# The last six expert tiles in half-tiles of tokens, with the next stage's norm and queries among them, in a four-stage transformer kernel

## The chip, the cores and the metric

One core of a Trainium2 chip runs the whole kernel in one launch. TensorE multiplies matrices into PSUM, VectorE, ScalarE and GpSimd work on tiles in SBUF, and SyncE (SP) issues most of the DMA copies. Waits between them are semaphores written out by hand. The metric is device time in microseconds, lower is better.

## The reference

Two layers, each an attention and a mixture of experts, on x of 4 batches x 256 tokens x 256 channels (1,024 tokens), all in float32:

```python
x = x + L0_xattn(layernorm(x), ctx, mask)    # dense attention on 1,601 context rows per batch
x = x + L0_ffn(layernorm(x), ...)            # 16 experts of width 176, 6 per token, plus a shared one of 352
x = x + L1_xattn(layernorm(x), ctx, mask)    # 16 heads of 16: q = Wq x + bq; softmax(clip(q k / 4)) v; Wo, norm
x = x + L1_ffn(layernorm(x), ...)            # 16 experts of width 128, 2 per token, plus a shared one
```

The change lies in the second line and its passage to the third. In L0_ffn every expert is computed for every token and scaled by that token's weight, which is zero where the expert was not chosen:

```python
for e in range(E):
    g = hs @ gate_proj[e].T; u = hs @ up_proj[e].T
    inter = silu(g) * u
    out = out + comb[:, e:e + 1] * (inter @ down_proj[e].T)
```

## The kernel before

**Precision.** A float32 product is made of three matmuls of split operands: high x high, high x low, low x high (mm3). Every operand exists as a rounded high part and the remainder. ScalarE usually writes the high part and VectorE subtracts for the low one.

**The feed-forward stage (ffn).** Its weights are 25 tiles of 128 hidden units: 3 of the shared expert (sh) and 22 of the experts (ex, NEX0). A tile holds gate, up and down weights, 768 columns. SP loads it into one of two slots of w_raw, and split on VectorE makes w_hi and w_lo of it, also in two slots: a copy, then a subtraction, then w_rdy counts one up. The 1,024 tokens are taken in two halves of 512. Half a tile is one chunk, numbered ct, 50 in all. For a chunk TensorE runs gate (6 matmuls of 512 columns) into bank 4 and up (6 more) into bank 5, and then down of the chunk before it (12 matmuls of 256 columns) into banks 0 to 3, where the whole stage's output is accumulated: banks 0 and 1 for the first half of the tokens, 2 and 3 for the second. Both halves of a tile come one after the other, so the banks of both are complete only at the last chunk. ScalarE takes silu of gate and later writes hh, the high part. VectorE multiplies silu by up (L1872), multiplies by the token's weight comb_b (L1876), subtracts for the low part hl (L1878), and in the first half of each tile then splits the next tile (L1796, L1798). comb_b has two slots; SP broadcasts a tile's weights into one (L426) as soon as the products of the tile two earlier are made. The expert tiles run in hardware loops of two tiles. Beside it SP fills x_slots in DRAM from blank with 20 copies of 1 MB (L416), one in each tile.

**The passage.** tiles_add adds a pair of output banks' halves to resid, then come statistics, the root (ScalarE's Sqrt and a reciprocal), tile_norm, transposes on TensorE (pair_T), and the split into xTh and xTl. This is done for the first two batches' tokens pair by pair. The first queries, of batch 0 and the first four heads, are made by first_queries with weights repeated three times over (wgh, wgl, made in attention_weights_lo), so that ScalarE and VectorE write them in place into qst. qst holds for every head high, high and low part and a row of ones on 49 partitions. All other queries are made for 512 tokens at a time (queries), written to qh and ql, and restacked into qst by DMA copies of 16 partitions that SP issues (restack, L536: 4 for each of three parts of a group of four heads), group by group, while the attention already runs. The second half's norm and queries run between the attention's units (early). SP issues the copies of keys (keys, kst), seven for a group of four heads, and of values (vsl) after the expert loop.

**The attention.** 208 units of 128 context rows for four heads: qk (L999), an exponential on ScalarE (L1483), a clip on VectorE (L2009), pv (L1041). The qk of the first unit waits for the keys and for the first queries.

Of the kernel before, what the change touches and what calls it, by code (L numbers as in the profile page):

```python
# [15 lines left out]
F32 = mybir.dt.float32  # L16
# [29 lines left out]
WC = 3 * D  # L46
EPS = 1e-5
# [32 lines left out]
def build(nc, a, out, stop="D"):  # L80
# [9 lines left out]
    with ExitStack() as ctx:  # L90
# [47 lines left out]
        with ExitStack() as s:  # L138
            Bt = lambda name, shape, dt=F32: sbuf(s, name, shape, dt)
            w_raw = Bt("w_raw", [P, 2, WC])  # L140
# [3 lines left out]
            w_hi = Bt("w_hi", [P, 2, WC], F32R)  # L144
            w_lo = Bt("w_lo", [P, 2, WC], F32R)
            silu = Bt("silu", [P, 2, 512])
            h32 = Bt("h32", [P, 2, 512])
            hh, hl = Bt("hh", [P, 2, 512], F32R), Bt("hl", [P, 2, 512], F32R)
            logit = Bt("logit", [E, NT * P])
            comb = Bt("comb", [E, NT * P])  # L150
            comb_b = Bt("comb_b", [P, 2, NT * P])
            g_s = Bt("g_s", [P, NT, E])
            g_c = Bt("g_c", [P, NT, E])
            g_pair = Bt("g_pair", [P, NT * 4, 6])
            g_gs = Bt("g_gs", [P, NT * 4])
            g_gr = Bt("g_gr", [P, NT * 4])
            g_beats = Bt("g_beats", [P, NT, E * (E + 1)])
            g_beats4 = Bt("g_beats4", [P, NT, 4 * 5])
            bar_w = Bt("bar_w", [P, MP], I32)
            bar_i, bar_f = bar_w[0:NB, :], bar_w[0:NB, :].bitcast(F32)  # L160
            Bt("gap3b", [P, 2032 - MP])
# [4 lines left out]
            blank = Bt("blank", [P, CAP // P, XW])  # L166

        with ExitStack() as s:
            C = lambda name, shape, dt=F32: sbuf(s, name, shape, dt)
            qst = C("qst", [P, NB, NH // 2, SEQ], F32R)  # L170
            p32 = C("p32", [P, PBUF, 1024])
            qh, ql = C("qh", [P, KT, NT * P], F32R), C("ql", [P, KT, NT * P], F32R)
            oS = C("oS", [P, SEQ])
            cx = C("cx", [P, NT, D])
            s4 = C("s4", [P, 2, HG])
            r4 = C("r4", [P, 2, HG])
            wq_raw = C("wq_raw", [P, KT, D])
            wo_raw = C("wo_raw", [P, KT, D])
            wqh, wql = C("wqh", [P, KT, D], F32R), C("wql", [P, KT, D], F32R)
            wgh, wgl = C("wgh", [P, KT, 2 * P], F32R), C("wgl", [P, KT, 2 * P], F32R)  # L180
            bq = C("bq", [P, KT])
            bq0 = C("bq0", [P, 2])
# [6 lines left out]
        with ExitStack() as s:  # L189
            Dt = lambda name, shape, dt=F32: sbuf(s, name, shape, dt)  # L190
            with ExitStack() as sw:
                yg = sbuf(sw, "yg", [P, NT, 2, D])
# [3 lines left out]
            Dt("gap5", [P, 5376])  # L196
# [32 lines left out]
            nv, na = Dt("nv", [P, 2]), Dt("na", [P, 2])  # L229
# [134 lines left out]
        def inverse_root(e, b, call):  # L364

            s = slice(2 * b, 2 * b + 2)
# [9 lines left out]
            link(e.tensor_scalar(nv[:], mv[:, s, 1], EPS, None, ALU.add))  # L376
            link(e.tensor_scalar(yi, nv[:].bitcast(I32), -0.5, 1597463007.0, ALU.mult, ALU.add))
            for k in range(3):
                link(e.tensor_tensor(na[:], nv[:], y, ALU.mult))
                link(e.tensor_tensor(na[:], na[:], y, ALU.mult))  # L380
                link(e.tensor_scalar(na[:], na[:], -0.5, 1.5, ALU.mult, ALU.add))
                if k < 2:
                    link(e.tensor_tensor(y, na[:], y, ALU.mult))
            e.tensor_tensor(rstd[:, s], na[:], y, ALU.mult).then_inc(rs_rdy, 1)

        @block.sync
        def _(sp):
# [16 lines left out]
            def load_rest(f):  # L404
                for k in range(2, f["sh"] + 1):
                    tile(f, 0, k)
                for r in range(f["ex"]):
                    if r + 1 < f["ex"]:
                        tile(f, 0, f["sh"] + r + 1)
# [9 lines left out]
                    e = f["e0"] + 2 * r  # L419
                    if e >= 4:  # L420
                        sp.wait_ge(mul2_rdy, e - 2)
                    edge = -(-r * P // f["width"]) * f["width"] - r * P
# [89 lines left out]
            if stop == "B":  # L512
                return store(sp)
# [45 lines left out]
            for job in range(KSL, NJ):  # L559
# [7 lines left out]
                if job == 2 * KSL:  # L567
                    ones_rows(2 * per, NB * per, q_in[NG])
# [1839 lines left out]
```

## Time and profile before

| | us |
|---|---|
| median of three runs | 740.78 |
| lowest, highest | 739.04, 744.77 |
| the profiled execution's own time | 739.67 |
| its span from first to last instruction | 737.8 |
| TensorE busy in the span | 683.4 (93%) |
| VectorE busy | 533.0 (72%) |
| ScalarE busy | 380.3 (52%) |
| GpSimd busy | 173.3 (23%) |

A busy time is the time in which an engine works on an instruction, waits left out. Matmuls are pipelined, so one that lasts 0.40 us is followed by the next after 0.23 us. The first stage takes up to about 185 us, the feed-forward from there to about 405, the attention from 414 to 632, the last stage the rest. The time of the execution is longer than the span by what lies before the first and behind the last instruction, 1.9 us.

### The profile page before, as it was taken

The numbers are of one execution on the slowest core, as the hardware profiler recorded it, in microseconds if no ns is written. First come the engines' busy times: TensorE is split into PE (matmuls) and PEld (weight loads), VectorE is DVE, ScalarE is ACT, GpSimd is POOL, SyncE is SP. The second block draws the span as 40 slices with busy tenths as digits, with TensorE's granted clock in tenths as the row PEclk, the third lists the DMA queues.
The fourth block names the chain that finished last, engine by engine and source line by source line (L and its number), as shares of the span: only waits on it lengthen the run. The fifth ranks groups of instructions, "written<-read, shape, count | busy, mean of one in ns | idle before, by whom it ended". The sixth has DMA issues, their size and how long they took to land.

```text
span 737.8 us, 14927 instructions
## 1 busy us (share of the span) xinstructions
PE 683.4 (93%) x5499; PEld 532.1 (72%) x5499; DVE 533.0 (72%) x1176; ACT 380.3 (52%) x566; POOL 173.3 (23%) x220
## 2 busy tenths in 40 slices
PE   4899999997999999999999799999999999989990
PEld 3899999996778888888887555454454554677870
DVE  5785767677566666666666788789789888775555
ACT  3634344431423223232233699999889999434550
POOL 4562727220010000000000050004204505343561
PEclk9999999999999999999999899999999999799996
DMA  7567475714437677776769859977979640654535
GB/s 253 183 208 263 155 268 170 270 68 149 149 117 261 215 225 254 244 240 215 219 217 212 126 79 173 181 149 107 213 125 195 112 69 2 214 215 135 167 125 192
DMA packets 55274, 131.55 MB, mean 178 GB/s; under 512 B 10006, under 2 KB 36102, under 8 KB 51630
## 3 DMA queue, kind: packets, MB, share of 16 engines
q1 hardware_dynamic: 51950, 123.32, 61.7%
q0 software_dynamic: 2256, 6.18, 2.4%
q10 hardware_dynamic: 1008, 1.25, 0.5%
q8 instruction: 38, 0.62, 0.4%
q14 instruction: 22, 0.18, 0.1%
HBM read 79.09 MB, written 48.82 MB: 173 GB/s over the span
## 4 chain that ended last, share of the span: by engine, by line
PE 74%; DVE 10%; POOL 5%; ACT 5%; DMA 3%; issue 3%; SPq 0%; ACTq 0%; DVEq 0%; POOLq 0%
PE ps L692 16%; PE ps L693 15%; PE ps L694 15%; PE ps L1041 10%; PE ps L999 7%; PE ps L1229 3%; ACT p L1483 2%; DVE p L2009 2%; PE ps L1245 2%; PE ps L1063 1%; PE ps L778 1%; DMA prob<-in_ctxT 1%; PE ps L1213 1%; POOL nv L376 1%; DMA comb_b<-comb_rows 1%
## 5 line engine op out<-in xcount | busy, mean ns | idle before, releaser
L1483 ACT ACTIVATE p<-ps 128x1024 f32<-128x1024 f32 (+1 forms) x208 | 193.4, 1052 | 9.8 <-PE ps L999 9.4
L2009 DVE TENSOR_SCALAR p<-p 128x1024 f32<-128x1024 f32 (+1 forms) x208 | 138.6, 686 | 18.5 <-ACT p L1483 17.6
L1041 PE MATMUL ps<-p,vsl 128*17 128x256 f32 (+1 forms) x1664 | 116.1, 383 | 6.6 <-DVE p L2009 5.3
L1389 ACT ACTIVATE hh<-h 128x512 fp32r<-128x512 f32 x50 | 31.6, 632 | 132.9 <-DVE h L1876 115.9
L999 PEld LDWEIGHTS ps<-qst,kst 49*128 49x128 f32 (+1 forms) x832 | 57.0, 182 | 48.3 <-issue 26.1
L376 POOL TENSOR_SCALAR nv<-mv 128x2 f32<-128x2 f32 x8 | 8.9, 1116 | 351.5 <-DVE mv L1939 210.5
L999 PE MATMUL ps<-qst,kst 49*128 49x256 f32 (+1 forms) x832 | 81.6, 311 | 1.3 <-DVE qst L1952 0.9
L692 PE MATMUL ps<-xTh,w_hi 128*128 128x512 f32 x200 | 79.9, 399 | 1.5 <-DVE h L1872 0.8
L693 PE MATMUL ps<-xTl,w_hi 128*128 128x512 f32 x200 | 79.0, 395 | 0.0
L694 PE MATMUL ps<-xTh,w_lo 128*128 128x512 f32 x200 | 78.9, 395 | 0.0
L1041 PEld LDWEIGHTS ps<-p,vsl 128*17 128x17 f32 (+1 forms) x1664 | 35.4, 96 | 47.0 <-DVE p L2009 12.6
L1878 DVE TENSOR_TENSOR hl<-h,hh 128x512 fp32r<-128x512 f32 x50 | 34.6, 692 | 36.6 <-ACT hh L1389 36.6
L692 PE MATMUL ps<-w_hi,hh 128*128 128x256 f32 x200 | 56.8, 284 | 1.8 <-DVE hl L1878 1.5
L1872 DVE TENSOR_TENSOR h<-silu,ps 128x512 f32<-128x512 f32 x50 | 34.4, 688 | 31.9 <-PE ps L694 20.8
L693 PE MATMUL ps<-w_lo,hh 128*128 128x256 f32 x200 | 56.3, 281 | 0.0
L694 PE MATMUL ps<-w_hi,hl 128*128 128x256 f32 x200 | 56.2, 281 | 0.0
L692 PEld LDWEIGHTS ps<-xTh,w_hi 128*128 128x128 f32 x200 | 37.7, 189 | 9.4 <-DVE h L1872 1.7
L694 PEld LDWEIGHTS ps<-xTh,w_lo 128*128 128x128 f32 x200 | 37.6, 188 | 8.9
L693 PEld LDWEIGHTS ps<-xTl,w_hi 128*128 128x128 f32 x200 | 37.7, 189 | 6.6
L692 PEld LDWEIGHTS ps<-w_hi,hh 128*128 128x128 f32 x200 | 37.7, 188 | 5.8 <-DVE hl L1878 3.8
L1342 ACT ACTIVATE prob<-sS,nmax 128x1602 f32<-128x1602 f32 x8 | 13.1, 1638 | 52.9 <-DVE nmax L1659 52.9
L1385 ACT ACTIVATE silu<-ps 128x512 f32<-128x512 f32 x50 | 29.8, 597 | 18.9 <-PE ps L694 18.2
(317 smaller groups left out, 1554.0 us busy)
## 6 DMA issues: line engine op xcount, KB each, us to landing
x_slots<-blank SPq DMA_DIRECT2D x20, 1032.0 KB, 5.9
kst<-k_hi SPq DMA_DIRECT2D x64, 200.2 KB
w_raw<-in_w SPq DMA_DIRECT2D x25, 384.0 KB, 3.6
v_one<-vst SPq DMA_DIRECT2D x4, 1768.0 KB, 7.8
vsl<-v_one SPq DMA_DIRECT2D x4, 1768.0 KB, 16.6
kst<-k_lo SPq DMA_DIRECT2D x32, 200.2 KB
e_w<-in_w SPq DMA_DIRECT2D x2, 3072.0 KB, 16.1
comb_b<-comb_rows SPq DMA_DIRECT2D x20, 256.0 KB, 5.7
```

The costliest lines, as they stand in the source:

```text
L692: e.matmul(o, lh, rh, start=first, stop=False, skip_group_check=True)
L693: e.matmul(o, lh, rl, start=False, stop=False, skip_group_check=True)
L694: return e.matmul(o, ll, rh, start=False, stop=last, skip_group_check=True)
L999: mm = pe.matmul(ps[0:rows, 2 * (x % RING) + t, c * SEQ:(c + 1) * SEQ], kst[r, job % KSL, c, m * P:m * P + rows], qst[r, b, 2 * g + c, :], ...
L1041: mm = pe.matmul(ps[32 * j:32 * j + VW, 6 + job % 2, 0:SEQ], vsl[0:rows, b % 2, at_:at_ + VW], p32[0:rows, x % PBUF, (2 * t + c) * SEQ:(2 ...
L1229: mm = pe.matmul(ps[:, 2 + j % 2, 0:2 * P], xbT[:, j % 2, k * P:(k + 1) * P], weights_of(j, slice(k * 2 * P, (k + 1) * 2 * P)), start=k == ...
L1385: act.activation(silu[:, half, :], ps[:, 4, :], ACT.Silu).then_inc(silu_rdy, 1)
L1389: act.activation(hh[:, half, :], h32[:, half, :], ACT.Copy).then_inc(hh_rdy, 1)
L1483: act.activation(p32[0:rows, x % PBUF, :], psf[0:rows, bank * 512:bank * 512 + 1024], ACT.Exp, scale=0.25).then_inc(p_exp, 1)
L1872: dve.tensor_tensor(h32[:, half, :], silu[:, half, :], ps[:, 5, :], ALU.mult).then_inc(mul1_rdy, 1)
L1878: dve.tensor_tensor(hl[:, half, :], h32[:, half, :], hh[:, half, :].bitcast(F32), ALU.subtract).then_inc(hl_rdy, 1)
L2009: dve.tensor_scalar(t, t, CLO, CHI, ALU.max, ALU.min).then_inc(p_clip, 1)
```

## The change

The last six expert tiles (KEEP = 6) are taken out of the loop. They run as twelve chunks: first the first half of the tokens for all six tiles, then the second half for all six. Their split weights are kept in six slots, so each is loaded and split once: w_hi, w_lo, w_hi2, w_lo2, w_hi3, w_lo3, placed where other stages' or the gate's buffers lie. The first half's output banks are complete when half of these chunks are done. Its addition, statistics, root (now on GpSimd, four tiles at once), norm, transposes and queries are put among the second half's chunks. first_queries and its weights wgh and wgl are gone: all queries go by qh, ql and restack. SP issues keys and values among the twelve chunks, and the 20 fillings of x_slots in the first 16 tiles. Batches 0 and 1 now lie in the upper half of qst, and the attention's units use the PSUM banks in the order 0, 4, 2. The diff, cut to its core:

```diff
@@ SP: copies @@
-                for r in range(f["ex"]):
-                    if r + 1 < f["ex"]:
-                        tile(f, 0, f["sh"] + r + 1)
+                for r in range(LOOP0):
+                    tile(f, 0, f["sh"] + r + 1)
...
-                    if 1 <= r <= NFILL:
-                        sp.dma_start(xs_d[(r - 1) * CAP:r * CAP, :].rearrange("(p k) d -> p k d", p=P), blank[:]).then_inc(x_zero, 16)
+                    for q in range((r - 1) * NFILL // (LOOP0 - 1) if r else 0, r * NFILL // (LOOP0 - 1)):
+                        sp.dma_start(xs_d[q * CAP:(q + 1) * CAP, :].rearrange("(p k) d -> p k d", p=P), blank[:]).then_inc(x_zero, 16)
...
+            def load_kept(f):
+
+                for e in range(2 * KEEP):
+                    half, k = e // KEEP, e % KEEP
+                    if e + 1 < KEEP:
+                        tile(f, 0, f["sh"] + LOOP0 + e + 1)
+                    sp.wait_ge(mul2_rdy, 2 * LOOP0 + e - (2 if e < 2 else 1))
+                    share(f, LOOP0 + k, e % 2, half * 512, half * 512 + 512)
+                    if e == KEEP - 1:
+                        keys(0)
+                    elif e == KEEP:
+                        values(0)
+                    elif KEEP < e < KEEP + KSL:
+                        keys(e - KEEP)
...
-            keys(0)
-            values(0)
-            keys(1)
-            keys(2)
...
+            load_kept(FFN["B"])
+
+            def queries(half, gs):
+                n = KT * half + gs[0] // 2
+                sp.wait_ge(q_hi, n + 1)
+                for g in gs:
+                    restack(half, g, 0)
+                    restack(half, g, 1)
+                sp.wait_ge(q_lo, n + 1)
+                for g in gs:
+                    restack(half, g, 2)
...
+            sp.wait_ge(q_hi, 1)
+            ones_rows(2 * per, NB * per, q_in[0])
+            queries(0, (0, 1))
+            queries(0, (2, 3))
@@ GpSimd: roots @@
-            pool.wait_ge(ln_mv, 3 * NT)
-            for b in range(2):
-                inverse_root(pool, 2 + b, b)
+            for h in range(2):
+                pool.wait_ge(ln_mv, 2 * NT + 4 * h + 4)
+                inverse_root(pool, 4 * h, 4 * h + 4, h)
@@ TensorE @@
+                for e in range(2 * KEEP):
+                    half, k = e // KEEP, e % KEEP
+                    ct = last + 1 + e
+                    gate(ct, tb + LOOP0 + k + 1, KEPT[k], half, False)
+                    if e == 2 * KEEP - 2:
+                        pair_T(0, 6)
+                        pair_T(1, 7)
+                    up(ct, KEPT[k], half, False)
+                    down(*prev)
+                    prev = (ct, KEPT[k], half, ct % 2)
+                    if e == 2 * KEEP - 2:
+                        pe.wait_ge(cw_rdy, 2)
+                        pe.wait_ge(ln_lo, 6)
+                        queries(0, 6)
+                queries(1, 7)
+                down(*prev)
...
-                    if b == 0 and g == 0:
-                        pe.wait_ge(q_lo, 4)
-                    elif b == 0:
-                        pe.wait_ge(q_in[g], 16 * (3 * HG + (1 if g % 2 else 0)))
+                    if b == 0:
+                        pe.wait_ge(q_in[g], 16 * (3 * HG + (g == 0)))
@@ ScalarE @@
+                for e in range(2 * KEEP):
+                    ct = c0 + 2 * (sh + LOOP0) + e
+                    near = e == 2 * KEEP - 2
+                    chunk(ct, ct % 2, mul2_rdy, 2 * LOOP0 + e + 1, between=tokens_hi if near else None)
+                    if near:
+                        act.wait_ge(x_zero, 16 * NFILL)
+                        queries_hi(0, 1, 6)
+                act.activation(std[:, 4:5], eps[:], ACT.Exp)
+                queries_hi(1, 2, 7)
@@ VectorE @@
-                with dve.Fori(0, ex // 2 - 1) as i:
-                    pair(i, False)
-                if n == 0:
-                    attention_weights_lo()
-                pair(ex // 2 - 1, True)
+                with dve.Fori(0, LOOP0 // 2) as i:
+                    pair(i)
+
+                first = c0 + 2 * (sh + LOOP0)
+                for e in range(2 * KEEP):
+                    half, k, ct, left = e // KEEP, e % KEEP, first + e, 2 * KEEP - e
+                    if left == 2:
+                        pair_lo(0, 6)
+                        pair_lo(1, 7)
+                    products(ct, half, ct % 2, True, e % 2, 16 * LOOP0 + 32 * (e // 2 + 1))
+                    if left == 6:
+                        tiles_add(0)
+                    elif left == 5:
+                        tiles_stat(0, 2)
+                    elif left == 4:
+                        attention_weights_lo()
+                    elif left == 3:
+                        dve.wait_ge(rs_rdy, 1)
+                        for t in range(4):
+                            tile_norm(t)
+                    low(ct, ct % 2)
+                    if e + 1 < KEEP:
+
+                        tn = tb + LOOP0 + k + 1
+                        if KEPT[k + 1] == 4:
+                            dve.wait_ge(v_out, 16 * NB)
+                        split(tn + 1, tn % 2, 16 * (tn // 2 + 1), first if KEPT[k + 1] == 0 else None, KEPT[k + 1])
+                    elif left == 6:
+                        tiles_add(1)
+                    elif left == 5:
+                        tiles_mean(0, 2)
+                    elif left == 4:
+                        residual_scale()
+                    elif left == 2:
+                        queries_lo(0, 1, 6)
+                queries_lo(1, 2, 7)
```

gate and up are the two parts of the former hidden; products and low those of the former chunk on VectorE (L1872 and L1876, and L1878). gate still waits for w_rdy when a tile's first half begins. share is the former broadcast of comb_b, for one half of the tokens.

## Rows read from the trace of the kernel before

**Rows 1.** Page, part 2: the clock granted to TensorE, 40 slices of 18.4 us.
```profile
PEclk9999999999999999999999899999999999799996
```

**Rows 2.** Busy time by stretches, granted clock (PEclk), DMA share and rate.
```profile
core 0: us, PE busy (x) PEld busy (x) DVE busy (x) ACT busy (x) POOL busy (x), PEclk, DMA share, GB/s
351.20:359.90 8.70, 8.70 (x51) 7.58 (x51) 5.66 (x9) 2.46 (x4) 0.00 (x0) 1.00 0.68 230
388.50:399.20 10.70, 10.70 (x61) 8.91 (x60) 7.83 (x13) 2.87 (x5) 0.00 (x0) 1.00 1.06 156
399.20:403.60 4.40, 3.16 (x20) 2.64 (x18) 2.01 (x4) 1.69 (x3) 0.00 (x0) 1.00 1.00 378
403.60:420.90 17.30, 12.94 (x68) 9.98 (x68) 13.08 (x30) 10.10 (x15) 0.00 (x0) 0.80 1.01 136
402.40:409.10 6.70, 2.35 (x16) 1.92 (x16) 5.47 (x17) 3.37 (x6) 0.00 (x0) 1.00 1.03 170
409.10:413.80 4.70, 3.71 (x18) 3.42 (x18) 3.47 (x9) 2.76 (x5) 0.00 (x0) 0.64 1.04 143
```

**Rows 3.** Timeline, TensorE, chunks 36 and 37: start, duration, engine, line.
```profile
345.28 0.40 PE L694 MATMUL ps<-xTh,w_lo 128*128 128x512 f32 x1
...
346.94 0.40 PE L692 MATMUL ps<-xTh,w_hi 128*128 128x512 f32 x1
...
349.50 0.40 PE L694 MATMUL ps<-xTh,w_lo 128*128 128x512 f32 x1
```

**Rows 4.** Timeline, VectorE, the same chunk: product, low part, split.
```profile
345.78 0.69 DVE L1872 TENSOR_TENSOR h<-silu,ps 128x512 f32<-128x512 f32 x1 [0.82 <-PE ps L694]
...
347.89 0.69 DVE L1878 TENSOR_TENSOR hl<-h,hh 128x512 fp32r<-128x512 f32 x1 [0.70 <-ACT hh L1389]
...
349.09 0.96 DVE L1798 TENSOR_TENSOR w_lo<-w_raw,w_hi 128x768 fp32r<-128x768 f32 x1
```

**Rows 5.** Timeline, the passage from the last down to attention unit 10.
```profile
403.90 0.39 PE L692 MATMUL ps<-w_hi,hh 128*128 128x256 f32 x1 [1.54 <-DVE hl L1878]
...
406.87 0.66 PE L930 MATMUL ps<-ident,xn 128*128 128x128 f32 x4 [1.27 <-DVE xn L1942]
...
413.74 1.13 PE L999 MATMUL ps<-qst,kst 49*128 49x256 f32 x8 [0.89 <-DVE qst L1952]
...
417.02 0.69 ACT L1424 ACTIVATE qh<-ps,bq 128x512 fp32r<-128x512 f32 x1 [0.79 <-PE ps L694]
...
423.52 3.77 ACT L1483 ACTIVATE p<-ps 128x1024 f32<-128x1024 f32 x4 [0.59 <-PE ps L999]
...
428.58 11.94 ACT L1483 ACTIVATE p<-ps 128x1024 f32<-128x1024 f32 x13 [0.16 <-PE ps L999]
```

**Rows 6.** Timeline, GpSimd: first and last of the 14 instructions of one root.
```profile
425.47 1.13 POOL L376 TENSOR_SCALAR nv<-mv 128x2 f32<-128x2 f32 x1 [210.54 <-DVE mv L1939]
...
430.72 0.55 POOL L384 TENSOR_TENSOR rstd<-na,rguess 128x2 f32<-128x2 f32 x1
```

**Rows 7.** Timeline, SP: issues of the values, of restacked queries and of ones.
```profile
390.28 0.39 SPq L527 DMA_DIRECT2D vsl<-v_one  x1
...
417.78 5.22 SPq L536 DMA_DIRECT2D qst<-qh  x8
423.04 3.11 SPq L536 DMA_DIRECT2D qst<-ql  x4
426.20 0.55 SPq L552 DMA_DIRECT2D qst<-ones  x1
```

**Rows 8.** DMA issues: size each, median us to landing; the last from 386 to 420.
```profile
x_slots<-blank SPq DMA_DIRECT2D x20, 1032.0 KB, 5.9
...
qst<-ql SPq DMA_DIRECT2D x28, 32.0 KB, 2.7
...
vsl<-v_one SPq DMA_DIRECT2D x1, 1768.0 KB, 15.7
```

More of the change, by code:

```diff
@@ L362, in store, with ring_bank, batch_at, w_at @@
             sp.wait_ge(out_done, 16)
-        def inverse_root(e, b, call):
-            s = slice(2 * b, 2 * b + 2)
+        def ring_bank(x):
+            return (0, 4, 2)[x % RING]
+        def batch_at(b):
+            return (b + NB // 2) % NB
+        def w_at(slot):
+            return ((w_hi, w_lo), (w_hi2, w_lo2), (w_hi3, w_lo3))[slot // 2]
+        def inverse_root(e, t0, t1, call):
+            s, w = slice(t0, t1), slice(0, t1 - t0)
             seen = [13 * call]
@@ L858, in weights_T, with gate @@
                     mm.then_inc(gT_rdy, 1)
-                def hidden(ct, tiles, slot, half, first):
+                def gate(ct, tiles, slot, half, first):
                     s = slice(half * 512, half * 512 + 512)
+                    wh, wl = (w[:, slot % 2, :] for w in w_at(slot))
                     if half == 0:
@@ L871, in hidden, with up @@
                         logits_T()
+                def up(ct, slot, half, first):
+                    s = slice(half * 512, half * 512 + 512)
+                    wh, wl = (w[:, slot % 2, :] for w in w_at(slot))
                     if not first:
@@ L875, in hidden, with down @@
                         w = slice(D + k * P, D + (k + 1) * P)
-                        mm = mm3(pe, ps[:, 5, :], w_hi[:, slot, w], w_lo[:, slot, w], xTh[:, k, s], xTl[:, k, s], k == 0, k == 1)
+                        mm = mm3(pe, ps[:, 5, :], wh[:, w], wl[:, w], xTh[:, k, s], xTl[:, k, s], k == 0, k == 1)
                     mm.then_inc(U_rdy, 1)
-                def down(ct, slot, half):
+                def hidden(ct, tiles, slot, half, first):
+                    gate(ct, tiles, slot, half, first)
+                    up(ct, slot, half, first)
+                def down(ct, slot, half, buf):
                     pe.wait_ge(hl_rdy, ct + 1)
-                    buf = half
+                    wh, wl = (w[:, slot % 2, :] for w in w_at(slot))
                     for j in range(4):
@@ L909, in step @@
                     pct = i * 4 + (2 * tb + 2 * j + half - 1)
-                    down(pct, slot if half else (tb + j - 1) % 2, (half + 1) % 2)
+                    down(pct, slot if half else (tb + j - 1) % 2, (half + 1) % 2, (half + 1) % 2)
                 for j in range(2):
@@ L1789, in ffn, with split @@
                 t0 = f["t0"]
-                def split(tn, slot, cnt, down=None):
+                def split(tn, slot, cnt, down=None, to=None):
+                    to = slot if to is None else to
+                    wh, wl = (w[:, to % 2, :] for w in w_at(to))
                     dve.wait_ge(w_in[slot], cnt)
@@ L1904, in ffn, with pair @@
                 tb = t0 + sh
-                def pair(i, last):
+                def pair(i):
                     for j in range(2):
```

288 lines of the change are left out of this document (105 added, 183 removed).

## The prediction

> **What bounds the kernel now.** I read the page's slices first: TensorE at its full clock nearly everywhere, one dip in the slice near 410 us [rows 1]. Then busy time by stretches: in the expert loop TensorE is busy for all of its 8.70 us a tile, so that stage goes by matmuls. From 402.4 to 409.1 us it works 2.35 of 6.70 us, and from 409.1 to 413.8 its clock is 0.64 on average, in part at the lower level of 1.2 GHz [rows 2]. That is the handover between the stages, which the change is about; the rest is not touched. So only the stretch from the loop's last but twelve half-tile to the attention's first units has to be worked out.
>
> Call a half-tile a chunk. Chunks are numbered 0 to 49, and T(c) is the end of chunk c's up matmuls. The change reorders chunks 38 to 49, called e = 0 to 11. TensorE's last up matmul ends at 345.28 + 0.40 = 345.68, the twelve matmuls of down follow until 346.94, and the next chunk's up ends at 349.50 + 0.40 = 349.90 = T(37) [rows 3]. A chunk is thus 4.22 us: down 1.43, gate 1.40, up 1.40. In VectorE's rows of the same tile the product starts 0.10 after T, the low part at T + 2.21, and the next tile's split ends at 349.09 + 0.96 = T + 4.37 [rows 4]. Before, another chunk of the same tile lies between that split and the gate that needs it.
>
> Unit 10 of the attention starts its exponential at 428.58 [rows 5], so before takes 428.58 - 349.90 = 78.7 us from T(37).
>
> **Part 1: the first halves (e = 0 to 5).** Here every chunk is a new tile. Its weights are split only behind the low part of the chunk ahead (split follows low on VectorE), and gate waits for w_rdy. Nothing but the down of the chunk ahead (1.43 us) lies in between. So the chain is: T, split ends at T + 4.37 [rows 4], handing over 0.10 (as from TensorE to the product), gate and up 11 x 0.233 + 0.40 = 2.96 [rows 3]. The period is 7.43 us, not 4.22. Five transitions (e = 0 to 1, up to 4 to 5): 5 x 3.21 = **+16.1 us**. e = 0 and all of e = 6 to 11 find their weights ready.
>
> TensorE then stands idle about 3 us in each 7.4 us. Nothing in the trace shows this pattern. A gap of 1.54 us [rows 5] left the clock at 1.00 (402.4 to 409.1), and a stretch with 2.35 of 6.70 us busy was followed by the half clock [rows 2]. Bounds: nothing, or gate and up at twice their time, 11 x 0.233 = 2.6 us for each of five. The gap is longer than the harmless ones, but the busy share, 57%, is nearer to full. I take 1.0 each: **+5** (0 to 13).
>
> **Part 2: the second halves.** e = 6 to 9 are 4 x 4.22. VectorE's additions there (adds, statistics, weights' low part, 0.7 to 1.5 us a chunk) fit in the 2.0 us a chunk that it has without a split. GpSimd's root for four tiles is priced as its root for two, 425.47 to 431.27 = 5.8 us [rows 6]; it begins about T(45) + 4.3 and is wanted at T(47) + 1.6 = T(45) + 10.0, so it costs nothing, or a few tenths.
>
> From T(47): down 1.43, gate 1.40, two pairs of transposes about 0.95 (0.66 for one pair alone [rows 5]), up 1.40, down 1.43, queries 1.40 with 0.25 to drain and hand over, ScalarE's write of the high part 0.69 [rows 5]: q_hi comes at T(47) + 9.0.
>
> **Part 3: what queries moves to SP.** Before, the first queries were written in place by ScalarE and VectorE. Now the first qk waits for group 0 restacked by copies, and SP issues for groups 0 and 1 together: ones rows 0.55, sixteen high copies at 5.22 / 8 = 0.65, then the four low ones of group 0 at 3.11 / 4 = 0.78 [rows 7], landing 2.7 us after issue [rows 8]: 0.55 + 10.4 + 3.1 + 2.7 = 16.8 us after q_hi. TensorE's remaining work there (gate, up, down, queries, down, some 7 us) hides under it; the copies end last. Then 0.54 to the first exponential (its ps is filled by the first four of the eight matmuls of 1.13 us at 413.74, so about half of that), ten of them at 3.77 / 4 = 0.94 [rows 5], and 1.5 us because TensorE has again been idle for some 10 us (the half-clock stretch before [rows 2] is the nearest row): 11.4 us.
>
> Sum without waits on copies: 4.22 + 5 x 7.43 + 4 x 4.22 + 9.0 + 16.8 + 11.4 = 95.5 us against 78.7: **+16.8**. In other words the handover itself, with its moved norm and queries, comes out about even (the transposes and queries no longer stand alone, the copies do), and part 1 is what is lost.
>
> **Part 4: copies in SP's queue.** Each chunk needs its share of comb_b. SP now issues keys(0) in e = 5, values(0) in e = 6, keys(1) in e = 7 and keys(2) in e = 8, each behind that chunk's share and ahead of the next. Before, values(0) was issued at 390.28 [rows 7] behind keys(0), and landed 15.7 us later [rows 8]; the rate is low while keys move (156 GB/s), jumps to 378 from 399.2 to 403.6, and falls to 136 until 420.9 [rows 2]. The queue is served in order, and keys(1) and keys(2) took 17.3 us together. After: T(43) = 349.90 + 4.22 + 37.15 = 391.3, its second product ends at 392.8, share 7 goes out, and keys(1) moves from about 395.5; with keys(2) that ends near 412.8. Share 9 is queued behind it, lands at 413.8, and is wanted at T(47) + 0.8 = 409.0: **+4.9** on products of e = 9, and all behind it (norm of the first half, pair_T, the queries) waits. That is a wait of TensorE of over 4 us inside e = 10, so the half clock is likely on the next matmuls: **+2** (0 to 4).
> The Trainium skill (DMA: Bandwidth & Descriptors, Queues, rings and completion order) says that each DMA engine consumes the descriptors of one ring in ring order, and that SP owns one ring on each; by it the share copies wait as here, and the rows agree.
>
> Nothing: fillings x_slots, twenty in fifteen steps. A step with two puts a second 5.9 us copy [rows 8] ahead of a share that has about 11 us from issue to use; cover gone, under 1 us for each of five steps. The dropped wgh copies of attention_weights_lo: VectorE had slack, 0.4 us at most.
>
> **Total**: 16.8 + 5 + 4.9 + 2 = 28.7 us on the profiled execution's 739.67, that is 768.4. The median of the runs is 1.1 higher, 740.78, so I say **769**.
>
> **Rivals.**
> (a) The share copies are not held up (keys move faster, or the queue serves both). For it: nothing but the higher rate of values. Then the 4.9 and the 2 go: 762.
> (b) The kept first halves run at the half clock: 2.6 x 5 in place of 5: 777. For it: the half clock at 409; against it: 57% busy.
> (c) The clock never falls in part 1: 764.
> (d) Weights are in time after all, so the reordering costs nothing: the 16.1 and the 5 go, 748; with share 9 in time as well 741. It needs the split to end 2.9 us sooner, at T + 1.43. Against it: the order in split and low. The middle, 745, is not slower by what can be told. This is the one on the other side.
> (e) The restacked copies are issued at 0.4 us each, as the copy of the values was (0.39 [rows 7]): 20 x 0.25 = 5 less, 764. To be faster than before it would take (d) too.
>
> **Chances.** About 1% (7.4 us) is what a measurement of this kernel can tell. Forecast 40%, (a) 18%, (b) 14%, (c) 12%, (d) 5%, (e) 7%, others 4%. Slower by over 1%: 94%; within 1%: 4%; faster: 2%. Low end: 16.8 alone with quick copies, 12 us, 753; high end: 16.8 + 13 + 4.9 + 4, and 3 for shares earlier than the ninth, 782.
>
> **What would show it.** The wait of TensorE's gate (xTh, w_hi2 and w_hi3) on VectorE's w_lo, five times, about 3 us. VectorE's product with comb_b in e = 9 waiting on a copy. qst copies 16 us long between the queries' write and the first qk, with TensorE idle. The clock by stretches. Wrong if products, not splits, come before gate; if w_lo ends before down does; or if the first qk starts within 8 us of the last down.

## The result, and the profile after

The changed kernel takes 769.33 us, the median of four runs (767.32 to 770.47); the kernel before took 739.91 us beside it. The ratio is 1.041, with a 95% interval of 1.037 to 1.045. The forecast was 769 us. One of the four runs of experiment 3 below, 769.65 us, was in a slower state of the chip and is left out of its median. The profiled execution took 767.32 us over a span of 765.5 us, 27.7 more than before, and the attention's last exponential begins 28.0 us later (658.24 against 630.25 us). The page's slices of the granted clock, 19.1 us each, show three slices below full in the passage (364 to 402 us, and the one at 440), where [rows 1] has one:

```profile
PEclk9999999999999999999789969999999999999995
```

The waits of the stretch from 350 to 450 us name where the passage lost its time. Columns: who waited for whom, us in total, times, longest:

```profile
PE ps L727 <- DVE w_lo L1815: 14.4, 5, 3.0
...
DVE h L1893 <- DMA comb_b<-comb_rows: 9.5, 2, 6.1
...
PE ps L1031 <- DMA qst<-ql: 8.4, 1, 8.4
...
PE ps L986 <- DVE xn L1990: 4.1, 1, 4.1
```

The first three have no like in the kernel before: five waits of gate for the low part of its weights, two of VectorE for its share of the router's weights, one of the first qk for the restacked queries. The fourth, the transposes' wait for the norm, was 1.3 us there [rows 5]; here it is a result of the second, since the norm stands behind that product on VectorE.

VectorE's timeline shows one period of the first halves, from one product (L1889) to the next. It answers to [rows 4]:

```profile
369.35 0.69 DVE L1889 TENSOR_TENSOR h<-silu,ps 128x512 f32<-128x512 f32 x1 [4.54 <-PE ps L729]
370.07 0.69 DVE L1893 TENSOR_TENSOR h<-h,comb_b 128x512 f32<-128x512 f32 x1
371.46 0.69 DVE L1897 TENSOR_TENSOR hl<-h,hh 128x512 fp32r<-128x512 f32 x1 [0.70 <-ACT hh L1421]
372.06 0.55 DVE L1813 CAST w_hi<-w_raw 128x768 fp32r<-128x768 f32 x1
372.65 0.96 DVE L1815 TENSOR_TENSOR w_lo<-w_raw,w_hi 128x768 fp32r<-128x768 f32 x1
379.26 0.69 DVE L1889 TENSOR_TENSOR h<-silu,ps 128x512 f32<-128x512 f32 x1 [5.65 <-PE ps L729]
```

The split ends at 373.61, 4.36 us after the up that began the period (369.25), and the next product starts 5.65 us later. That is where TensorE works off gate and up, at 2.96 us at full clock [rows 3] and at more than that here. By stretches, as in [rows 2] (the first five are the five periods, the sixth is e = 6 to 9, then the wait for share 9, the work behind it, and the wait for the restacked queries):

```profile
core 0: us, PE busy (x) PEld busy (x) DVE busy (x) ACT busy (x) POOL busy (x), PEclk, DMA share, GB/s
352.90:360.50 7.60, 4.61 (x27) 3.86 (x26) 3.50 (x5) 1.23 (x2) 0.00 (x0) 1.00 0.22 76
360.50:369.30 8.80, 5.81 (x26) 4.70 (x25) 3.50 (x5) 1.23 (x2) 0.00 (x0) 0.82 0.26 83
369.30:379.20 9.90, 7.14 (x26) 5.77 (x26) 3.50 (x5) 1.23 (x2) 0.00 (x0) 0.67 0.22 68
379.20:388.10 8.90, 6.27 (x26) 5.18 (x26) 3.50 (x5) 1.23 (x2) 0.00 (x0) 0.77 0.66 128
388.10:397.10 9.00, 6.00 (x26) 4.84 (x25) 3.50 (x5) 1.23 (x2) 0.00 (x0) 0.81 0.91 256
397.10:414.00 16.90, 16.90 (x96) 14.42 (x95) 9.65 (x21) 3.69 (x6) 2.80 (x14) 1.00 0.89 143
414.00:424.40 10.40, 4.50 (x19) 3.38 (x18) 4.15 (x9) 1.45 (x3) 0.00 (x0) 0.83 0.80 127
424.40:428.00 3.60, 3.27 (x13) 2.98 (x14) 2.85 (x6) 1.98 (x4) 0.00 (x0) 0.55 0.25 73
...
440.00:449.00 9.00, 1.65 (x12) 1.39 (x12) 0.50 (x1) 0.90 (x1) 0.00 (x0) 0.57 0.23 51
```

VectorE's products with the share for e = 8 and e = 9, each with its wait in brackets:

```profile
413.99 0.69 DVE L1893 TENSOR_TENSOR h<-h,comb_b 128x512 f32<-128x512 f32 x1 [3.42 <-DMA comb_b<-comb_rows]
...
423.34 0.69 DVE L1893 TENSOR_TENSOR h<-h,comb_b 128x512 f32<-128x512 f32 x1 [6.09 <-DMA comb_b<-comb_rows]
```

SP's issues in the passage, which answer to [rows 7]: share 7, the six copies and the bar row of keys(1), share 8, later the ones rows, sixteen high copies and eight low ones:

```profile
398.64 0.79 SPq L451 DMA_DIRECT2D comb_b<-comb_rows  x2
399.47 0.42 SPq L558 DMA_DIRECT2D kst<-k_hi  x1
...
402.27 0.53 SPq L561 DMA_DIRECT2D kst<-bar_rows  x1
402.86 1.12 SPq L451 DMA_DIRECT2D comb_b<-comb_rows  x2
...
432.30 0.61 SPq L589 DMA_DIRECT2D qst<-ones  x1
432.95 10.28 SPq L573 DMA_DIRECT2D qst<-qh  x16
443.27 5.04 SPq L573 DMA_DIRECT2D qst<-ql  x8
```

And ScalarE's part of it, the write of the queries' high part and the first exponentials (units 0 to 5, then 6 to 12), as in [rows 5]:

```profile
431.53 0.69 ACT L1457 ACTIVATE qh<-ps,bq 128x512 fp32r<-128x512 f32 x1 [0.74 <-PE ps L729]
...
448.10 5.60 ACT L1504 ACTIVATE p<-ps 128x1024 f32<-128x1024 f32 x6 [9.58 <-PE ps L1031]
454.41 6.60 ACT L1504 ACTIVATE p<-ps 128x1024 f32<-128x1024 f32 x7 [0.70 <-PE ps L1031]
```

Unit 10 is the fifth of the last group and begins at 454.41 + 4 x 0.94 = 458.2.

### The profile page after: what moved, and what is told of

The parts are those of the page before. It is cut to its first block, busy times and chain, and to the rows that moved or that the text cites. A ratio compares the mean times of both kernels' runs of the same rounds, so it can differ in the third digit from the quotient of the medians.

```text
span 765.5 us, 14809 instructions
## 1 busy us (share of the span) xinstructions
PE 688.9 (90%) x5475; PEld 536.4 (70%) x5475; DVE 529.1 (69%) x1160; ACT 375.6 (49%) x559; POOL 172.7 (23%) x220
## 4 chain that ended last, share of the span: by engine, by line
PE 68%; DVE 11%; DMA 5%; POOL 5%; ACT 5%; issue 3%; SPq 3%; ACTq 0%; DVEq 0%; POOLq 0%
PE ps L727 14%; PE ps L729 13%; PE ps L728 13%; PE ps L1071 9%; PE ps L1031 6%; PE ps L1259 4%; DMA comb_b<-comb_rows 3%; ACT p L1504 2%; PE ps L1275 2%; DVE p L2030 2%; SPq L573 1%; PE ps L1093 1%; PE ps L813 1%; DVE h L1889 1%; ACT hh L1421 1%
## 5 line engine op out<-in xcount | busy, mean ns | idle before, releaser
L727 PE MATMUL ps<-xTh,w_hi 128*128 128x512 f32 x200 | 83.8, 419 | 15.9 <-DVE w_lo L1815 14.4
L398 POOL TENSOR_SCALAR nv<-mv 128x2 f32<-128x2 f32 (+1 forms) x8 | 8.7, 1083 | 381.6 <-DVE mv L1987 238.8
L1031 PE MATMUL ps<-qst,kst 49*128 49x256 f32 (+1 forms) x832 | 83.6, 316 | 9.2 <-DMA qst<-ql 8.4
L729 PE MATMUL ps<-xTh,w_lo 128*128 128x512 f32 x200 | 82.4, 412 | 0.0
L728 PE MATMUL ps<-xTl,w_hi 128*128 128x512 f32 x200 | 82.1, 410 | 0.0
L1889 DVE TENSOR_TENSOR h<-silu,ps 128x512 f32<-128x512 f32 x50 | 34.4, 688 | 53.4 <-PE ps L729 44.4
L727 PEld LDWEIGHTS ps<-xTh,w_hi 128*128 128x128 f32 x200 | 39.7, 198 | 25.4 <-DVE w_lo L1815 15.4
L729 PEld LDWEIGHTS ps<-xTh,w_lo 128*128 128x128 f32 x200 | 39.6, 198 | 9.7
L728 PEld LDWEIGHTS ps<-xTl,w_hi 128*128 128x128 f32 x200 | 39.8, 199 | 7.2
L728 PEld LDWEIGHTS ps<-w_lo,hh 128*128 128x128 f32 x200 | 38.6, 193 | 2.2
## 6 DMA issues: line engine op xcount, KB each, us to landing
kst<-k_hi SPq DMA_DIRECT2D x64, 200.2 KB
vsl<-v_one SPq DMA_DIRECT2D x4, 1768.0 KB, 14.3
kst<-k_lo SPq DMA_DIRECT2D x32, 200.2 KB
```

The source lines that it names most:

```text
L727: e.matmul(o, lh, rh, start=first, stop=False, skip_group_check=True)
L728: e.matmul(o, lh, rl, start=False, stop=False, skip_group_check=True)
L729: return e.matmul(o, ll, rh, start=False, stop=last, skip_group_check=True)
L1031: mm = pe.matmul(ps[0:rows, ring_bank(x) + t, c * SEQ:(c + 1) * SEQ], kst[r, job % KSL, c, m * P:m * P + rows], qst[r, batch_at(b), 2 * g ...
L1889: dve.tensor_tensor(h32[:, buf, :], silu[:, buf, :], ps[:, 5, :], ALU.mult).then_inc(mul1_rdy, 1)
```

## The experiments

All of them change the order of the changed kernel's work, and leave its computation whole. Times are medians; a ratio is to the kernel before, timed beside it. That kernel had medians from 736.33 to 739.91 us in the five sessions of these runs, so a difference between medians of different sessions (1 to 4; 5 to 7; 8 and 9; 10; the changed kernel's own) is good to some 3 us. "First exponential" is the start of unit 0, 448.10 in the changed kernel's trace.

**1. The split one tile earlier.** VectorE splits the weights of kept tile e + 2, not e + 1, behind the low part of chunk e; tile 1 is split before the first kept chunk.

```diff
+                keep(1)
                 for e in range(2 * KEEP):
...
                     low(ct, ct % 2)
-                    if e + 1 < KEEP:
-                        tn = tb + LOOP0 + k + 1
...
-                        split(tn + 1, tn % 2, 16 * (tn // 2 + 1), first if KEPT[k + 1] == 0 else None, KEPT[k + 1])
+                    if e + 2 < KEEP:
+                        keep(e + 2)
```

> One part of the change altered: each kept tile is split one tile earlier on VectorE (tile 1 ahead of the twelve chunks, tile e + 2 behind the low part of chunk e). Nothing else moves. The theory (gate waits for the split of its own tile, and the half clock in this stretch comes from these gaps): the five waits of gate on w_lo (14.4 us) go to nearly nothing, the clock there is 1.00, and the five periods of 7.5 to 9.9 us (44.2 us) become some 4.4 each, 22 us less. A part comes back, because keys(0), values(0), keys(1), keys(2) are now issued in less time ahead of the shares: the waits on comb_b grow from 9.5 us to 12. 749 us (745 to 754). The rival, that the weights' load or the share of the token weights holds the first halves, and not the split's place: no change, 769.

Measured: 758.44 us, ratio 1.026 (1.019 to 1.033), 10.9 below the changed kernel where 20 were expected, and above the expected range. The waits on w_lo are gone from the stretch, and the five periods take 4.49, 4.50, 4.50, 4.50 and 3.00 = 21.0 us (products at 354.39 and 375.38) instead of 44.2. That is 23.2 us less, where 22 were expected. But the waits on the shares doubled:

```profile
DVE h L1893 <- DMA comb_b<-comb_rows: 20.4, 4, 7.5
```

The first exponential is at 436.82, 11.3 us earlier. So half of what the split gave was taken back further on: SP's queue has the same keys and values to move in less time, and now holds up four shares.

**2. The split between the product and the low part.** The first halves then keep a shorter wait.

```diff
                     products(ct, half, ct % 2, True, e % 2, 16 * LOOP0 + 32 * (e // 2 + 1))
-                    if left == 6:
+                    if e + 1 < KEEP:
+                        keep(e + 1)
+                    elif left == 6:
                         tiles_add(0)
```

> A dose of the same: the split of the next tile stands between the products and the low part of a chunk, not behind the low part, so it ends at about T + 3.1 in place of T + 4.4. The theory: each of the five waits of gate shrinks from 3.0 to about 1.7 us, the low part (at T + 3.1 to 3.8) still comes before down wants it; with the clock mostly full a period is 5.9 us, 29.5 for five against 44.2. Less what the shares take back: 756 us (752 to 762). If the wait were on something else than the split: 769.

Measured: 759.91 us, ratio 1.027 (1.019 to 1.035), within its range. The waits on w_lo are 8.1 us in five, 1.6 the longest; the period is 6.11 us throughout, and the product waits 2.38 us for TensorE, against 5.65 above. The granted clock from 355.0 to 385.5 us is 1.00. The waits on shares are 15.1 us in three.

```profile
367.15 0.69 DVE L1889 TENSOR_TENSOR h<-silu,ps 128x512 f32<-128x512 f32 x1 [2.38 <-PE ps L729]
...
373.26 0.69 DVE L1889 TENSOR_TENSOR h<-silu,ps 128x512 f32<-128x512 f32 x1 [2.38 <-PE ps L729]
```

**3. keys(1) and keys(2) behind the restack.**

```diff
                     elif e == KEEP:
                         values(0)
-                    elif KEEP < e < KEEP + KSL:
-                        keys(e - KEEP)
...
             queries(0, (0, 1))
+            keys(1)
+            keys(2)
```

> One part undone: keys(1) and keys(2) are issued behind the restacked queries of groups 0 and 1, not among the twelve chunks. The theory (the shares stand behind the keys in SP's queue): the two waits of VectorE's product on comb_b, 3.4 and 6.1 us, go, T(47) to q_hi falls from 18.2 to about 9.3 us, nothing waits for keys(1) 12 us into the attention: 760 us (758 to 763). The rival, that the shares are late for their own latency or SP's issue: the waits stay, 769.

Measured: 762.93 us (three runs, 757.3 to 766.72), inside its range, ratio 1.030 (1.019 to 1.041): an interval that reaches to the changed kernel's own, so by times alone the gain, 6.4 us, isn't certain. (With the fourth run the median is 764.83, 4.5 below the changed kernel; the expectations of experiments 5 and 6 reckon with that.) The traces are clearer: no wait on comb_b is left, the first exponential is at 439.90, 8.2 us earlier, and the span is 761.1, only 4.4 shorter. A new wait on keys, which was expected not to come, appears 14 us into the attention:

```profile
PE ps L1031 <- DMA kst<-bar_rows: 1.9, 1, 1.9
```

**4. Group 0 of the queries restacked whole before group 1.**

```diff
-            queries(0, (0, 1))
+            queries(0, (0,))
+            queries(0, (1,))
```

> Only the order of SP's restack issues is changed: all twelve copies of group 0, then group 1's. The theory (the first qk waits for the last copy of group 0, at 0.64 us an issue): eight high copies fewer ahead of it, so the 8.4 us wait of the first qk on qst shrinks by 5.1 to about 3.3: 764 us (763 to 766). The rival, that the copies' landing (some queue behind the keys) and not their issue is the cost: less than 2 us.

Measured: 763.53 us, ratio 1.031 (1.025 to 1.038). The wait of the first qk goes from 8.4 to 3.3 us, exactly the eight issues of 0.64 us that no longer stand ahead of it, and the time is inside its range. The first exponential is 6.6 us earlier, at 441.50; the span of the profiled execution is only 1.7 shorter, since the attention took 215.0 us there instead of 210.1.

**5. Edits 1 and 3 together.**

> Two edits together: the split of a kept tile one tile earlier, and keys(1), keys(2) issued behind the restack of group 0 and 1. Theory (the advance of the split was eaten by the share copies standing behind the key copies): the 20.4 us of waits on comb_b go to under 5 us (keys(0) and values(0) still stand ahead of shares 6 and 7), both gains come in whole, 23 us and 8 us off the passage, the first exponential of the attention at about 427 us, some 3 us of it given back to later waits on the keys: 741 us (736 to 748). Rival (the two gains overlap, the first halves of the six tiles are then held up by something else, such as the half clock or the low part): the sum of what each gave alone, 10.9 + 4.5: 754 us (750 to 758), with the first exponential at about 432 us or later.

Measured: 746.84 us, ratio 1.012 (1.008 to 1.017), inside the theory's range and below the rival's. The two gains are more than the sum of the single ones: 22.5 us against 10.9 + 6.4 = 17.3. That difference lies within the interval of experiment 3; the traces carry the point. The waits on comb_b are 5.4 us in two, and the first exponential is at 421.25, 26.8 us earlier, where the single edits gave 11.3 and 8.2. So the split's missing gain did go to the queue. The first exponential came 6 us sooner than expected, the time did not: the attention took 215.0 us, 4.9 longer than in the changed kernel.

**6. Edits 1, 3 and 4 together.**

> All three edits together: split a tile earlier, keys(1) and keys(2) behind the queries, group 0 of the queries restacked whole before group 1. Theory (the three costs stand one behind the other on one path): 5 us below the kernel with the first two edits, the wait on the restack (qst) 3.3 us, the first exponential at about 422 us: 737 us (731 to 744), so the same as the kernel before within 1%. Rival (single gains only: 10.9 + 4.5 + 5.8): 748 us (745 to 752).

Measured: 750.05 us (746.28 to 753.61), ratio 1.015 (1.011 to 1.020). A miss for the theory. The time lies in the rival's range, but not for the rival's reason, that each edit keeps its single gain: it is no faster than without edit 4. The wait on qst fell by its 5 us and the first exponential came at 416.34, but the next job's keys, issued behind the restack at 422.27, were then late:

```profile
PE ps L1032 <- DMA kst<-bar_rows: 5.3, 1, 5.3
```

What was gained was lost in the attention: from its first to the start of its last exponential it takes 643.67 - 416.34 = 227.3 us, against 658.24 - 448.10 = 210.1 in the changed kernel. Of the 17.2 us the wait itself is 5.3. Most of the rest goes with the clock, as the stretches show for TensorE:

```profile
416.00:440.00 24.00, 18.22 (x152) 9.40 (x153) 11.44 (x23) 14.39 (x16) 4.87 (x14) 0.57 0.78 107
424.00:428.00 4.00, 4.00 (x38) 1.63 (x28) 2.87 (x9) 2.53 (x3) 2.94 (x8) 0.50 1.08 149
436.00:440.00 4.00, 4.00 (x36) 1.79 (x38) 0.69 (x1) 2.07 (x3) 0.00 (x0) 0.50 1.03 127
440.00:460.00 20.00, 19.83 (x256) 10.35 (x252) 16.89 (x36) 18.60 (x21) 0.00 (x0) 0.94 1.06 151
```

The clock is at the lower of its two levels on both sides of the wait for keys, which ends at 435.55. From 416 to 428 us it follows the wait for the queries; there two exponentials are followed by 1.05 us in which ScalarE waits for TensorE. So not all of the low clock comes from the late keys.

**7. keys(1) ahead of the restack.** As 6, but keys(1) is issued right behind the last share, and only keys(2) behind the queries.

```diff
             load_kept(FFN["B"])
+            keys(1)
...
             queries(0, (0,))
             queries(0, (1,))
-            keys(1)
             keys(2)
```

> As the kernel with all three edits, but keys(1) is issued right behind the last share, ahead of the restack, and only keys(2) behind it. Theory: keys(1) takes about 9 to 11 us of the queue's bytes, the restack's first copy is issued some 9 us later, so they meet only in part; the wait on kst in the attention (about 2 us where keys(1) and keys(2) both came late) goes: 736 us (730 to 744), 0 to 2 us below the kernel with all three edits. Rival (the restack is small and sits behind 200 KB of keys in the DMA engines): the wait on qst grows from 3.3 to 6 us or more and the time is 2 to 4 us above the kernel with all three edits.

Measured: 741.56 us (twelve runs, 737.39 to 742.81), ratio 1.0035 (1.001 to 1.006): 8.5 us below experiment 6 (12.9 by the spans of the profiled executions), where at most 2 were expected. The first exponential did not move (416.82), nor did the wait on qst (3.3), so the gain all comes from the attention: 213.8 us from the first to the last exponential, 13.5 less than in 6. The rival (the restack held up by the keys' bytes) is out. By ScalarE's timelines, unit 30 of the attention begins 39.4 us behind unit 0 in experiment 6 and 30.1 in 7; the other 4.2 of the 13.5 us come later, with two further dips of the clock in experiment 6 (0.83 from 460 to 480 us, 0.86 from 520 to 540), whose cause no run shows. The profiled executions also lie at opposite ends, 751.27 us in the upper part of experiment 6's range and 738.36 in the lower part of this one's (737.39 to 742.81); the medians differ by 8.5. The wait on keys, which was expected to go, is not gone altogether: one of 1.7 us is left 39 us into the attention. What is left ahead of it is

```profile
DVE h L1894 <- DMA comb_b<-comb_rows: 5.3, 2, 2.8
```

**8. keys(0) and values(0) into the first halves.** As 7, but keys(0) goes in three pieces behind shares 1, 2 and 3, where the DMA engines are about half idle (a share of 0.40 to 0.49 between 350 and 370 us of experiment 7), and values(0) behind share 5.

```diff
-                    if e == KEEP - 1:
-                        keys(0)
-                    elif e == KEEP:
-                        values(0)
+                    if 1 <= e < 4:
+                        keys(0, ((0, 1), (2, 3), (4, 5, 6))[e - 1])
+                    elif e == KEEP - 1:
+                        values(0)
```

> As the kernel that has the early split, keys(1) behind the last share, keys(2) behind the queries and group 0 restacked first (741.6 us), but keys(0) is issued in three pieces behind shares 1 to 3 and values(0) behind share 5. Theory: the two waits on comb_b that are left there (2.8 and 2.5 us) come from keys(0) and values(0), of which only values(0) still stands ahead of a share: the waits go from 5.3 to about 2.5 us or less, the first exponential of the attention from 416.8 to about 414 us, the time to 739 us (736 to 742). Rival: in the first halves the tile's transfer and the share need the queue, the pieces hold shares 2 to 4 or the weights, a new wait of 2 us or more appears before 376 us, and the time stays at 741 to 744 us.

Measured: 733.76 us (731.08 to 734.85), ratio **0.992 (0.989 to 0.995)**: below the expected range, 35.6 us below the changed kernel and 5.6 below the kernel before in the same session. The interval leaves out 1, though the prediction took 1% as what a measurement can tell. From 352 to 403 us the only wait on a copy that is left is one of 0.4 us. TensorE never stops between the products of e = 0 and e = 9:

```profile
353.60:391.80 38.20, 38.20 (x214) 32.54 (x213) 28.11 (x48) 10.62 (x18) 3.79 (x13) 1.00 0.67 166
```

The first exponential is at 410.94 and unit 10 at 417.25 + 4 x 0.93 = 421.0, where before had 428.58 [rows 5]. The first exponential came 5.9 us sooner than in experiment 7 and the span is 4.8 us shorter; the medians, which are of different sessions, differ by 7.8.

**9. Four of the restacking copies on ScalarE.** As 8, with the second high block of group 0 issued by ScalarE between the last SiLU and the last copy of h.

```diff
+            def restack_part1():
...
+                act.wait_ge(q_hi, 1)
+                for c in range(2):
+                    for t in range(2):
...
+                        act.dma_start(qst[at_:at_ + HD, batch_at(0):batch_at(0) + 2, c, :].bitcast(F32),
...
-                    restack(half, g, 1)
+                    if half or g:
+                        restack(half, g, 1)
```

> As the kernel with keys(0) early, and four of the twelve copies that restack group 0 of the queries (its second block of high parts) are issued by ScalarE, in its idle time of 2.3 us behind the SiLU of chunk 47, instead of by SyncE. Theory: each issue costs SyncE 0.65 us and the path runs through SyncE's issues, so the last low copy is issued 2.6 us earlier: 736.5 us (733 to 740), 2 to 3 us below the kernel with keys(0) early, the wait on qst from 3.3 us to about 1 us. Rival (the issues cost ScalarE more than its idle time, and the copy of h's high part for chunk 47 comes late, or the low part of the queries is then what ends last): within 1 us of the kernel with keys(0) early.

Measured: 734.05 us (twelve runs, 729.72 to 739.17), ratio 0.992 (0.989 to 0.995): no change that can be told from experiment 8: the number the rival gave. SP is done with the low copies of group 0 at 407.03 instead of 408.88, counted from the ones rows 5.87 us instead of 8.40, but the wait of the first qk fell from 3.3 to 2.5 us only. Counted from the ones rows the first qk begins at 9.39 us instead of 9.93: the copies were issued 2.5 us sooner and landed 0.5 us sooner. The other 0.3 of the wait is TensorE's own work ahead of it, which ended later. keys(1) is still moving at that time (DMA share 1.05 from 397 to 403 us); that the small copies stand behind it is the likely reason, and was not tried by itself. ScalarE's copy of h for chunk 49 stood 2.56 us behind its SiLU instead of 2.32, which is that 0.3: the rival's reason, at a tenth of the issue time saved. The Trainium skill (DMA: Bandwidth & Descriptors, Rules for kernel authors) says that spreading copies over several issuing engines gives no bandwidth and only saves the sequencer's issue time. The trace agrees: 2.5 us of issue saved, 0.5 us at the reader.

**10. Experiment 8 with the split back in its place.**

> The kernel of 733.8 us (all moved copies: keys(0), values(0), keys(1), keys(2) and group 0 of the restack) with the split of a kept tile put back where the change has it, behind the low part. It prices the split's place by itself, with nothing on the queue to eat the gain. Theory (prediction's step on the first halves, 16.1 us, plus the fall of the clock there, which the changed kernel's trace put at 7): the five waits of 2.9 us on w_lo are back, the granted clock of the stretch falls to about 0.8, and the time is 733.8 + 23 = 757 us (753 to 761). Rival (the gain of 23 us was partly a gain of the moved copies): below 750 us.

Measured: 758.77 us, inside its range, ratio 1.028 (1.020 to 1.036). The split's place is worth 25.0 us by the medians (27 by the ratios) when nothing downstream takes the gain back. The five periods take 46.7 us (products at 355.43 and 402.10) against 21.0 in experiment 8: 16.1 for the waits at full clock, as predicted, and 9.5 for the clock. Over them

```profile
355.33:402.00 46.67, 32.34 (x122) 26.27 (x122) 17.50 (x25) 6.13 (x10) 0.00 (x0) 0.74 0.41 116
```

The last column is the attention, from the start of its first exponential to the start of its last.

| kernel | median, us | first exponential, us | waits on w_lo / shares / qst, us | attention, us |
|---|---|---|---|---|
| before | 739.91 | 414.28 | none | 216.0 |
| changed | 769.33 | 448.10 | 14.4 / 9.5 / 8.4 | 210.1 |
| 1, split earlier | 758.44 | 436.82 | 0 / 20.4 / 8.4 | 211.9 |
| 2, split between | 759.91 | 441.59 | 8.1 / 15.1 / 8.4 | 212.2 |
| 3, keys later | 762.93 | 439.90 | 14.4 / 0 / 8.3 | 215.5 |
| 4, group 0 first | 763.53 | 441.50 | 14.7 / 8.5 / 3.3 | 215.0 |
| 5, 1 and 3 | 746.84 | 421.25 | 0 / 5.4 / 8.3 | 215.0 |
| 6, 1, 3 and 4 | 750.05 | 416.34 | 0 / 5.7 / 3.3, keys 5.3 | 227.3 |
| 7, keys(1) ahead | 741.56 | 416.82 | 0 / 5.3 / 3.3 | 213.8 |
| 8, keys(0) early | 733.76 | 410.94 | 0 / 0.4 / 3.3 | 213.4 |
| 9, four copies on ScalarE | 734.05 | 411.09 | 0 / 0 / 2.5 | 211.3 |
| 10, 8 without 1 | 758.77 | 438.20 | 14.3 / 0 / 3.3 | 213.3 |

The changed kernel's attention is the shortest, so of a gain at the first exponential 1 to 5 us are missing again at its end in the others, and 17 in experiment 6. Waits on keys (1.7 to 2.9 us in experiments 3, 7, 8 and 10) are a part of that; for the rest no run shows a cause. The kernel before is no mark here: its first ten exponentials took 14.3 us, the changed kernel's 10.0.

## Why the prediction was right

The 769 us were the sum of six terms. The path T(37) to unit 10 measures 458.2 - 348.7 = 109.5 us; the sum had 107.4, so it is 2.1 us longer than said. T(37) came 1.2 us earlier than before, and about 1.6 us were regained inside the attention, which brings the span to its 27.7 us.

**Part 1, right in its mechanism and its size.** A period of 7.43 us was worked out from rows in which it did not occur. The first one, still at full clock, is 7.50 us (products at 353.04 and 360.54). Experiments 1 and 10 show that the cause is the split's place behind the low part and nothing else; rival (d), weights in time, is out.

**The clock there, too small.** The term was 5 us. The five periods sum to 44.2 us against 5 x 7.43 = 37.15, so it is 7.0 here and 9.5 in experiment 10 (46.7). The first period, with 4.61 of 7.60 us busy, ran at the full clock; the next four at 0.67 to 0.82. The bounds, 0 and 13, held it. The argument from the busy share was no better than a guess, since like periods were granted different clocks: rivals (b) and (c) were both wrong, the truth lay between them, as chosen. Experiment 2 shows a milder pattern, gaps of 1.6 us, without any loss.

**Part 2, right.** e = 6 to 9 kept their 4.22 us (16.90 for four, TensorE never idle), under all of VectorE's additions and GpSimd's root; the norm waited for a share, never for the root, which took 3.9 us (409.36 to 413.23) and not 5.8.

**Part 4, the mechanism right, the size off by 3.6.** Share 9 was to be 4.9 us late, and was 8.5: it landed at 423.3 and was wanted at T(47) + 0.8 = 414.8. The step that failed is the time of keys(1) and keys(2), taken as 17.3 us from before [rows 2]. From the issue of keys(1) at 399.47 to the landing of share 9 it took 23.8 us. In the two stretches from 397.1 to 424.4, 16.90 x 143 + 10.40 x 127 = 3.7 MB were moved, and before in its 17.3 us 17.3 x 136 = 2.35 MB. The sizes in the view of issues account for it: two sets of keys are 2.5 MB (twelve copies of 200.2 KB and two of 25), and four shares (7 to 10) of 0.26 MB are 1.05; before the first key copy was issued, 0.15 MB of values(0) were still moving. So what the sum left out is in the main the time of shares 7 and 8, which stand before and between the keys: an estimate from the mean rate of this stretch, 137 GB/s, is 1.9 us a share, where the sum had 1.0 for share 9 alone. From there to the 3.6: 23.8 less 17.3 is 6.5, of which 1.0 was in the sum for share 9's own landing, and the 23.8 begin 2.4 us after T(43) (397.1), where the sum's 17.3 began 4.2 after it; that gives 3.7. Share 8 was late too, by 3.4 us, which the sum did not have; it cost nothing of its own, because share 9 came later still. So the wait's total in the view, 9.5 us, is not its price. Experiment 3 put the price at 8.2 us of the passage.

**The clock behind share 9, too large.** It was to cost 2 us. From T(47) to the high part of the queries it took 432.22 - 413.98 = 18.2 us; less 9.0 and 8.5 this leaves 0.7. The clock did fall, to 0.83 from 414.0 to 424.4 and 0.55 from 424.4 to 428.0, but was back at full from there. Experiment 3, without the wait, took 8.7 us for the 9.0.

**Part 3, a little too large.** The first qk came at 447.27, 15.1 us after the queries' high part instead of 16.8: the issues cost 0.64 and 0.63 us each, not 0.65 and 0.78, and the last copy landed 2.1 us after the start of its issue. The sum had 2.7 for that and added it to the end of the issue, which counted one issue, 0.63 us, twice. Rival (e), 0.4 us each, is out. The chain of 10.9 us to unit 10 was forecast at 11.4.

So of the six terms two were short by 2.0 and 3.6 us and three long by 1.3, 1.7 and 0.5: the agreement to a third of a microsecond is luck; the single terms were right to 4 us and their sum to 2.1.

**What the prediction did not say.** That its terms do not add when they are taken away one by one. Taken out of the changed kernel singly, the three costs give 10.9, 6.4 and 5.8 us by the medians; the split and the keys together give 22.5 rather than 17.3, and at the first exponential 26.8 rather than 11.3 + 8.2 = 19.5. A gain upstream of a busy queue is lost to the queue; a queue's gain upstream of the attention is lost to late keys.

## What to carry to other kernels

Before moving work to where "each piece is new", look for the operation that prepares the next piece and where it stands in its engine's order: here a 1.5 us split, made in the chunk just before it was wanted instead of one earlier, cost 25 us, more than all else together. A removal that gives less than its wait promised is worth a second look at what stands next on the path; the remedy here was two edits together, 10.9 and 6.4 us alone and 22.5 as a pair. When small urgent copies and large patient ones share a queue, put the large ones where the queue is idle, not merely later: keys(1) behind the restack cost 8.5 us that it did not ahead of it, and the early places brought the change to 0.8% below the kernel before.

## What the runs showed of the hardware

Repeated gaps of 3 us cost more than one gap would suggest: TensorE busy 4.61 of 7.60 us had the full clock, and the four like periods behind it were granted 0.82, 0.67, 0.77 and 0.81, values between 1.2 GHz (0.50) and 2.4 GHz (1.00), so the clock changed level within each. Which period falls is not fixed: in experiment 10 the same pattern was granted 0.81, 0.81, 0.67, 0.67 and 0.77, from the first period on. With gaps of 1.6 us in 6.11 there was no loss (1.00, experiment 2).

A slow clock in the attention isn't hidden: with the full clock, TensorE is busy for 178.12 of the 182.00 us from 458 to 640 in the changed kernel's trace. Behind the wait for the queries the attention began at 0.50 in the three traces read for it (448 to 452 us in the changed kernel, 416 to 424 in experiment 6, 416.5 to 424 in 7). The wait of 5.3 us in experiment 6 brought the clock back to 0.50 (436 to 440 us): unit 30 of its attention began 9.3 us later behind unit 0 than in experiment 7.

A copy that is issued sooner need not land as much sooner: 2.5 us at the issue gave 0.5 us at the reader, with keys in flight (experiment 9).
